# The layer norm's last step on ScalarE instead of VectorE, in the middle stage of a transformer layer

## What is computed

```python
out = out.transpose(1, 0, 2, 3).reshape(bsz, seq_len, H * HD)   # num / den, 16 heads of 128
return out @ Wo.T

def _layernorm(x, axis=-1, eps=1e-05):
    m = jnp.mean(x, axis=axis, keepdims=True)
    v = jnp.var(x, axis=axis, keepdims=True)
    return (x - m) / jnp.sqrt(v + eps)

x = _layernorm(x + _L0_attn_ref(x, ...), axis=-1)
x = _layernorm(x + _L0_ffn_ref(x, ...), axis=-1)     # begins with fwht(x * SU_ug) / SCALE
```

## Time and profile before

| | us |
|---|---|
| median of 3 runs | 2736.41 |
| lowest, highest | 2734.31, 2740.14 |
| the profiled execution | 2734.8 |
| its span, first to last instruction | 2733.1 |

### The profile page before, as it was taken

How to read it: one execution, slowest core, us unless ns; L and a number is a source line. 1 busy time by engine, 2 the same in 40 slices (tenths; PEclk the granted TensorE clock), 3 DMA queues, 4 the chain that set the end, 5 groups by cost and what they waited for, 6 DMA issues and landing times. The chain is left out here.

```text
span 2733.1 us, 32657 instructions
## 1 busy us (share of the span) xinstructions
PE 2531.1 (93%) x10689; PEld 1938.5 (71%) x10689; DVE 1680.8 (62%) x2275; ACT 1043.4 (38%) x1820; POOL 831.2 (30%) x669
## 2 busy tenths in 40 slices
PE   5899999999999999959999977999999999999997
PEld 3566666666666666638777766888888888888886
DVE  7587878787878787866767754443434343434444
ACT  2455555555555555532333323322222222222221
POOL 4365656565656565622322320000000000000000
PEclk8899999999999999979999998999999999999999
DMA  6111010101010101056666523310101010000000
GB/s 218 38 36 50 35 54 31 50 35 50 31 54 31 54 31 54 32 209 235 227 233 225 217 93 131 116 47 1 46 0 46 0 46 15 31 15 31 15 31 15
DMA packets 85163, 198.79 MB, mean 73 GB/s; under 512 B 8320, under 2 KB 25728, under 8 KB 74112
## 3 DMA queue, kind: packets, MB, share of 16 engines
q1 hardware_dynamic: 85120, 198.24, 20.4%
HBM read 134.77 MB, written 63.44 MB: 73 GB/s over the span
## 5 line engine op out<-in xcount | busy, mean ns | idle before, releaser
L1193 DVE SCALAR_TENSOR_TENSOR th<-th,pgu 128x512 f32<-128x512 f32 x128 | 88.1, 689 | 413.6 <-ACT th L1136 413.5
L1241 POOL TENSOR_TENSOR rstdc<-vec,neghalfc 128x1 f32<-128x1 f32 x32 | 17.5, 548 | 1063.0 <-DVE vec L1181 1063.0
L1136 ACT ACTIVATE th<-pgu,sg 128x512 f32<-128x512 f32 x128 | 88.1, 688 | 479.3 <-PE pgu L1074 479.3
L605 POOL TENSOR_TENSOR tb<-tb,sinb 128x512 f32<-128x512 f32 x160 | 221.1, 1386 | 132.5 <-ACT tb L489 131.7
L772 PE MATMUL py<-woh,oh 128*128 128x512 f32 x512 | 205.9, 402 | 28.2 <-DVE ol L885 28.2
L609 POOL TENSOR_TENSOR Ql<-tb,Qh 128x512 fp32r<-128x512 f32 x128 | 181.8, 1426 | 116.8 <-ACT Qh L498 116.8
L1074 PE MATMUL pgu<-x2h,wgh 128*128 128x512 f32 x512 | 200.7, 392 | 15.8 <-DVE x2l L1223 15.8
L422 PE MATMUL pj<-xh,wqh 128*128 128x512 f32 x512 | 208.0, 406 | 4.3 <-DVE ta L536 4.3
L493 ACT ACTIVATE tb<-ta 128x512 f32<-128x512 f32 x160 | 100.9, 631 | 269.5 <-DVE ta L540 269.1
L772 PE MATMUL py<-woh,ol 128*128 128x512 f32 x512 | 202.5, 395 | 0.0
L772 PE MATMUL py<-wol,oh 128*128 128x512 f32 x512 | 202.2, 395 | 0.0
(11 more groups left out here) (187 smaller groups left out, 6068.7 us busy)
## 6 DMA issues: line engine op xcount, KB each, us to landing
num_scratch<-no SPq DMA_DIRECT2D x128, 256.0 KB, 2.4
nt<-num_scratch SPq DMA_DIRECT2D x32, 1024.0 KB, 5.3
rb<-rden_scratch SPq DMA_DIRECT2D x32, 1024.0 KB, 6.0
x2st<-x_scratch SPq DMA_DIRECT2D x36, 256.0 KB, 3.6
xst<-in_xT SPq DMA_DIRECT2D x35, 256.0 KB, 3.7
xr<-in_x SPq DMA_DIRECT2D x32, 256.0 KB, 5.5
x_scratch<-x SPq DMA_DIRECT2D x32, 256.0 KB, 5.6
x_scratch<-x SPq DMA_DIRECT2D x8, 1024.0 KB, 4.3
```

The lines of the kernel that those rows point to most:

```text
L605: nc.gpsimd.tensor_tensor(tb[s][:, :], tb[s][:, :], sinb[:, :], ALU.mult).then_inc(sin_done, 1)
L1136: nc.scalar.activation(th[s][:, :], pgu[2 * s][:, :], ACT.Tanh, scale=sg[:, f:f + 1]).then_inc(tanh_done, 1)
L1193: nc.vector.scalar_tensor_tensor(out=th[s][:, :], in0=th[s][:, :], scalar=1.0, in1=pgu[2 * s][:, :], op0=ALU.add, op1=ALU.mult).then_inc(g ...
L1241: nc.gpsimd.tensor_tensor(rstd[:, :], ve[:, :], neghalf[:, :], ALU.pow).then_inc(rc_done, 1)
```

## The change

`norm` goes from VectorE's list to ScalarE's, ahead of `columns`. Instead of (x - mean) * rstd with two operands per row on VectorE, ScalarE computes rstd * x + shift as one activation of the function Identity, where shift = -mean * rstd. VectorE negates the mean in place (one instruction of one element per row, ahead of `ve`), and GpSimd multiplies it by `rstd` into the new tile `shift`, after the power and behind a wait for it. `rstd_done` now rises by two for each chunk. VectorE waits for the product of the chunk before ahead of writing `mv` anew; GpSimd waits for the norm of the chunk before ahead of writing `rstd` anew.

```diff
+        shift = sb("shift", [P, 1])
@@ ScalarE
+            def norm(s, n):
+                act.wait_ge(rstd_done, n * 2 + 2)
+                nc.scalar.activation(x1[s][:, :], x1[s][:, :], ACT.Identity, scale=rstd[:, 0:1],
+                                     bias=shift[:, 0:1]).then_inc(x1_ready, 1)
...
                 if at >= 1:
+                    norm(1 - s, n - 1)
                     columns(1 - s, (j - 1) % NCH, n - 1, m * 4 - 2 if j == 1 and at >= NCH else None)
...
+            norm(1, NC - 1)
             columns(1, NCH - 1, NC - 1, None)
@@ VectorE
                 dve.wait_ge(ln_step, n * 3 + 1)
+                if at >= 1:
+                    dve.wait_ge(rstd_done, n * 2)
                 nc.vector.sem_inc(passed, 1)
                 nc.vector.bn_aggr(mv[:, :], stats[:, :]).then_inc(ln_step, 1)
                 dve.wait_ge(ln_step, n * 3 + 2)
+                nc.vector.tensor_scalar_mul(mv[:, 0:1], mv[:, 0:1], -1.0)
                 nc.vector.tensor_scalar_add(ve[:, :], mv[:, 1:2], EPS).then_inc(ln_step, 1)
-
-            def norm(s, n):
-                dve.wait_ge(rstd_done, n + 1)
-                nc.vector.tensor_scalar(x1[s][:, :], x1[s][:, :], mv[:, 0:1], rstd[:, 0:1], ALU.subtract,
-                                        ALU.mult).then_inc(x1_ready, 1)
...
-                if at >= 1:
-                    norm(1 - s, n - 1)
...
-            norm(1, NC - 1)
@@ GpSimd
                 pool.wait_ge(ln_step, n * 3 + 3)
+                if not isinstance(n, int) or n:
+                    pool.wait_ge(x1_ready, n)
                 nc.gpsimd.tensor_tensor(rstd[:, :], ve[:, :], neghalf[:, :], ALU.pow).then_inc(rstd_done, 1)
+                pool.wait_ge(rstd_done, n * 2 + 1)
+                nc.gpsimd.tensor_tensor(shift[:, :], mv[:, 0:1], rstd[:, :], ALU.mult).then_inc(rstd_done, 1)
```

## The result

The changed kernel takes 2748.5 us (median of 6) against 2735.4 us (median of 6) for the kernel before: ratio 1.0048, 95% interval 1.0035 to 1.0061. It is slower by 13 us, not by the 36 that were forecast. The profiled execution has a span of 2746.4 us, 13.3 more than that of before.

What follows compares the result with a forecast made beforehand. TensorE, busy 93% of the span, was taken as the bound, so only its waits count. Ordinary steps +36, j = 3 steps -2, clock +1 and tail +1 made +36 us: forecast 2772 us, range 2748 to 2804.

Steps and rivals of the forecast that it cites:

- the forecast's own case: Second stage: the transposes wait for a norm delayed by the held product; chance 0.72, spanning 2752 to 2795 us.
- 1, `lower` starts later: Ordinary second-stage step: negating the mean ahead of `ve` starts `lower` 0.10 us later, not hidden.
- 8, from the last sum to the end: Tail: the last chunk has no `lower` or `divide`; 0.1 + 0.55 + 0.2 make 1 us more.
- Step 3: Ordinary step: GpSimd's product is held until `divide` ends, finishing 6.90 to 7.31 us after the sum, taken as 7.1.
- step 2: Ordinary step: with the norm off VectorE, `divide` directly follows `lower`, starting at 4.20 and ending at 6.49 to 6.90 us.
- Step 5: Ordinary steps: transposes start at 7.95 instead of 6.42, a 1.5 us stall; 24 steps cost 36 us (22 to 44).
- step 4: Norm as ScalarE activation with two operands per row: estimated 0.75 us (0.63 to 0.85), running 7.14 to 7.89.
- Step 7: TensorE's granted clock: seven long gaps go (up to 6 us back), 24 short ones come (12 us); taken as plus 1.
- step 6: j = 3 steps with `xsl`: waits total 2.5 us instead of 2.8, seven times, 2 us gained (between 0 and 16).
- VectorE keeping its turn: Rival: VectorE holds the turn over instructions without a gap, delaying power and product; 68 us more, 2804 us; chance 0.10.
- the product slips in: Rival: the product gets in before `divide` reads, norm done at 6.1; 2716 to 2732 us, say 2720; chance 0.12.

Runs made afterwards that it cites:

- divide waits: Changed kernel with one more VectorE wait: `divide` waits for GpSimd's product of the chunk; 2714.9 us, ratio 0.9928 to the kernel before.
- lower waits: Changed kernel with one more VectorE wait: `lower` waits for GpSimd's product, so power and product run first; 2711.8 us, ratio 0.9923 to the kernel before.
- norm first: Kernel before with two calls exchanged: VectorE does the norm ahead of `lower`; 2717.1 us, ratio 0.9930.
- transposes later: Kernel before, with TensorE's transposes in j = 3 steps after the thirteenth head instead of the tenth; 2717.5 us, ratio 0.9925.

## Why the prediction was off

The direction was right, and so was the mechanism in all but the clock; the sum was nearly three times too large. The measured 2748.5 us is inside the stated range (from 2748) by 0.5 us only, and below the forecast's own case, which began at 2752. By the prediction's own steps:

| step | forecast us | measured us |
|---|---|---|
| 1, `lower` starts later | 0.10 a step | 0.12 in j = 0 and 1 (0.04 of it the negation), 0 in j = 2 |
| 2, end of `divide` | 6.49 to 6.90 | 6.50 |
| 3, end of the product | 7.1 | 6.55 |
| 4, the activation | 0.75 | 0.81 |
| 5, stall in an ordinary step | 1.5 | 1.20, 1.04, 0.85 (j = 0, 1, 2) |
| 5, ordinary steps together | +36 | +23.8 |
| 6, waits in j = 3 | -2 | -4.1 |
| 7, the clock | +1 | -6.2 |
| sum of 5 to 7 | +35 | +13.5 |
| 8, from the last sum to the end | +1 | +0.4 |

- Step 3 is the one that failed most. I put the product at 0.55 us alone and 0.41 behind a turn, both taken from the power, and let a cheaper multiplication count only for the lower end. It is 0.19 alone and 0.05 behind the turn. The second power in its place, which ended 0.41 behind and cost 10.7 us more, shows that this is the whole difference of the two: 0.36 us a step, 8.6 us in the 24 steps of the forecast.
- In step 2 I gave half of 0.41 us to a delay of `divide`, 4.9 us in 24 steps. There is none. I had the row for that (`lower` at 2.29 us beside the power, rows 5) and did not follow it.
- Step 5 took the one cover of 6.42, of j = 1, for all steps; it is 6.33 in j = 0 and 6.60 in j = 2. And 23 steps wait, not 24, for in the last j = 2 step nothing holds the product for long (0.70 us).
- In step 4 two operands per row cost more than 57 ns each: 813 ns against the 631 of the copy with constants is 91 for each. The 57 came from two rows that differ in more than the operand: the one of 688 is a Tanh that reads PSUM, the one of 631 a copy that reads SBUF. The measured 813 ns lies beside the 799 of the page "ScalarE: Activation LUTs" of the Trainium skill (section What ACT_TABLE_LOAD costs): the page was nearer than my estimate from rows.
- Step 7 had the wrong sign, 7.2 us off. I let 24 short gaps cost clock drops, up to a third of them, by the first stage's example. None did. And I held the return of the drops in the long gaps for an "up to". They all came back, since step 6 splits the long gap into two short ones, of 0.69 and 1.03. The first stage was no example of short gaps: its mean wait of 1.4 us hides two kinds. Of the 34 waits for `Sl` between 200 and 1200 us 16 are under 1 us and 18 are 1.74 to 2.65, and each of the 11 stretches at the lower clock between 200 and 1190 us lies beside a single gap of 1.7 to 2.6 us. One of them, with the stretch around it, in the kernel before:

```profile
444.93 0.80 PE L456 MATMUL pnum<-Qh,Sh 128*128 128x512 f32 x1 [2.62 <-DVE Sl L581]
...
440.00:450.00 10.00, 7.38 (x22) 4.10 (x20) 8.74 (x14) 5.15 (x10) 6.04 (x6) 0.72 0.14 52
```

- Step 6 was right in its order (`xsl` behind the product, then a second wait of 1.0) and gave 0.5 a step instead of 0.3, as the product ended earlier. It said seven waits of 2.80; there were six, and the listed gap of the last j = 3 step was 0.71.
- Of the rivals, VectorE keeping its turn is refuted: the product was served between `divide` and `xb` in every step that has them (j = 1: it ends at 6.55, `xb`, begun at 6.42, at 7.64). The order of issue says the same as the alternation there, since the product was issued at 4.79; no run tells the two apart. That the product slips in came about only when VectorE was made to wait, and then brought about what was worked out for it: 2714.9 us, or 2716.7 by the ratio on the forecast's 2736.4, where 2716 to 2732 stood for a product in front of `divide`.
- The waiting rule of the page "SBUF — State Buffer" of the Trainium skill (section Summary: rules for kernel authors) held wherever GpSimd's instruction came second: 0.19 us of product became 1.76. Where a short GpSimd instruction came first it did not show: the power of rows 5 was issued 0.15 ahead of `lower` and ran 0.40 into it, and `lower` took its usual 2.29. There the measurement decides.

## What to carry to other kernels

A GpSimd instruction that is issued while VectorE runs a long instruction with two inputs in SBUF cost here its wait until that one's end, plus its own work; price the own work by the same operation, not by one of the same shape. When an instruction is taken from an engine, ask what its wait did for others: VectorE's wait for the power was the window in which GpSimd worked, and moving the norm closed it. Where an engine has room, put that wait back, or order its list so that the short chain runs ahead of the long two-input instructions: here that was worth 1.2 to 1.3% on the changed kernel, and it came out 0.7 to 0.8% below the kernel before. A mean of waits says nothing about single gaps: look at the gaps one by one before giving them a price in clock.

## What the runs showed of the hardware

- A GpSimd instruction of one element per row, served between two VectorE instructions that stand back to back, didn't lengthen the second one: `divide` at 2.28, `xb` at 1.22 us. A long one did: `divide` 6.66, `lower` 6.58 behind `xsl`.
- Between two long instructions that come for the turn together, the one issued first went first, by as little as 0.07 us: `xsl` ahead of the norm (by 0.07), of `divide` (0.08) and of `lower` (0.17); without the product `divide` was issued 0.46 ahead of `xsl` and went first.
- TensorE's clock and single gaps (listed lengths) of the second stage's j = 3 steps: at 2.46 us four of six had a stretch at 1.2 GHz, at 1.79 three of six; at 1.43 and below none in any step of seven kernels (changed, second power, divide waits, lower waits, norm first, transposes later, no negation). A drop cost 1.5 to 1.6 us. With the norm back on VectorE and gaps of 2.85 to 2.88 us, five of six such steps were long (17.8 to 19.3 us) and one was not (16.59); four of these drops cost 1.4 to 1.6 us and one 2.75. In the first stage of the kernel before, 11 of 19 single gaps of 1.7 us and more had one beside them, the two of 1.1 and 1.5 had none. What decides in a given step stays open.
